# Around the first leaf of a blocked factorisation: the last key sums earlier, the upper columns of T cleared by ScalarE, three places for a

## The reference

```python
def attn(x, ...):                      # x: 8 batches, 1024 tokens, 256 wide; H = 128
    Q, K, V = x@Wq.T+bq, x@Wk.T+bk, x@Wv.T+bv
    def step(carry, qkv):              # scan over the 1024 tokens
        A, M = carry                   # A starts as the identity, M as zero, both HxH
        q, k, v = qkv
        s_t = sum(k * q)
        u = k / (norm(k) + 1e-6)
        Au = A @ u
        denom = 1.0 + u @ Au
        A = A - outer(Au, Au) / denom
        z = Au / denom
        M = M + outer(v, s_t * z)
        return (A, M), M @ q
    return scan(step) @ Wo.T + bo
x = x + 0.5 * ffn(layernorm(x))        # ffn: ternary weights, 256 -> 1024 -> 256, exact gelu
x = x + attn(layernorm(x))
x = x + 0.5 * ffn(layernorm(x))
```

## Time and profile before

| | |
|---|---|
| median of 3 runs | 1112.4 us (1110.78 to 1113.61) |
| the profiled execution | 1110.24 us, its span 1108.5 us |
| busy: PE, DVE, ACT, POOL | 940.0, 792.9, 532.3, 301.5 us |
| mean granted clock of PE | 0.917 of full speed |
| HBM read, written | 49.16 MB, 37.75 MB |
| key blocks, up to the last product of the last block | 0 to 312.7 us |
| first leaf, from `take` to `turned` | 319.86 to 369.94 us |
| second leaf | 376.85 to 419.39 us |
| third, fourth leaf | 428.0 to 470.6, 480.3 to 522.8 us |
| second part of the program | from 537.7 us |

### The profile page before, as it was taken

One profiled execution on the slowest core, in us unless ns is written; L12 is line 12 of the kernel. 1 busy time (PEld: TensorE's weight loads), 2 busy tenths in 40 slices (PEclk: granted clock), 3 DMA queues, 4 the chain that ended last, 5 costly groups with the idle time before them and its releaser, 6 DMA issues.

```text
span 1108.5 us, 28517 instructions
## 1 busy us (share of the span) xinstructions
PE 940.0 (85%) x11675; PEld 724.5 (65%) x11675; DVE 792.9 (72%) x2503; ACT 532.3 (48%) x1093; POOL 301.5 (27%) x256
## 2 busy tenths in 40 slices
PE   4799999999985877577899546692799999999998
PEld 1467777777773756465797435582667777777766
DVE  6877777777667897968359797886366666566663
ACT  4678788787733133112226212101175666566574
POOL 4345353535210000000000000000664654546340
PEclk9999999999998788778999686896799999999999
DMA  5353547545236463244443000057542433424231
GB/s 154 67 133 98 152 114 191 119 138 139 85 120 191 124 138 104 59 118 115 109 130 106 3 3 4 4 155 155 152 91 73 106 96 82 120 67 106 57 77 58
DMA packets 185522, 113.98 MB, mean 103 GB/s; under 512 B 85808, under 2 KB 178352, under 8 KB 184752
## 3 DMA queue, kind: packets, MB, share of 16 engines
q1 hardware_dynamic: 168496, 95.38, 34.1%
q10 hardware_dynamic: 16896, 16.78, 4.9%
HBM read 49.16 MB, written 37.75 MB: 78 GB/s over the span
## 4 chain that ended last, share of the span: by engine, by line
PE 32%; DVE 15%; issue 2%; DMA 1%; POOL 1%; ACT 1%; SPq 0%; DVEq 0%; ACTq 0%; POOLq 0%
PE ldl_work L2027 10%; PE ldl_work L2015 10%; DVE ldl_lane_matrix L1151 6%; DVE ldl_rank_one L1148 4%; DVE lane_rows L1133 2%; PE ldl_work L1999 2%; DVE ldl_lane_dinv L1136 2%; PE ldl_work L1594 2%; PE ldl_work L1604 1%; PE ldl_work L1982 1%; PE ldl_work L1990 1%; PE ldl_work L1983 1%; PE ldl_work L1969 1%; PE ldl_work L1411 1%; PE ldl_work L1404 1%
## 5 line engine op out<-in xcount | busy, mean ns | idle before, releaser
L1780 POOL TENSOR_TENSOR T<-T,out_bv_rows 128x512 f32<-128x512 f32 x16 | 20.3, 1272 | 430.5 <-DMA out_bv_rows<-in_bqkv 424.3
L445 DVE TENSOR_TENSOR ffn_h_rest<-ffn_ps_h,ffn_h_high 128x512 f16<-128x512 f32 x128 | 86.2, 684 | 56.1 <-ACT ffn_ps_h L616 55.6
L615 ACT ACTIVATE ffn_h_high<-ffn_ps_h,b_columns 128x512 f16<-128x512 f32 x128 | 87.9, 687 | 64.6 <-PE ffn_ps_h L694 64.1
L2027 PE MATMUL ldl_work<-w_ternary,ldl_panels 128*128 128x256 f16 x512 | 118.2, 273 | 0.0
L708 PE MATMUL ffn_ps_y<-w_ternary,ffn_h_rest 128*128 128x256 f16 x512 | 117.8, 273 | 0.0
L708 PE MATMUL ffn_ps_y<-w_ternary,ffn_h_high 128*128 128x256 f16 x512 | 117.8, 273 | 0.0
L694 PE MATMUL ffn_ps_h<-ffn_xT_high,w_ternary 128*128 128x512 f16 x256 | 98.7, 385 | 11.8 <-DVE ffn_h_rest L445 11.8
L694 PE MATMUL ffn_ps_h<-ffn_xT_rest,w_ternary 128*128 128x512 f16 x256 | 98.3, 384 | 0.0
L2015 PE MATMUL ldl_work<-out_xT_high,w_ternary 128*128 128x512 f16 x256 | 97.0, 379 | 0.0
L2015 PE MATMUL ldl_work<-out_xT_rest,w_ternary 128*128 128x512 f16 x256 | 97.0, 379 | 0.0
L1928 ACT ACTIVATE ldl_work<-ldl_work,b_columns 128x512 f32<-128x512 f32 x128 | 84.2, 658 | 0.0
(11 more groups left out here) (215 smaller groups left out, 2301.3 us busy)
## 6 DMA issues: line engine op xcount, KB each, us to landing
ffn_x<-in_x SPq DMA_DIRECT2D x16, 512.0 KB, 4.7
x_scratch<-ffn_x_out ACTq DMA_DIRECT2D x16, 512.0 KB, 3.3
aT_scratch<-ffn_aT SPq DMA_DIRECT2D x16, 512.0 KB, 5.0
inv_aT<-aT_scratch SPq DMA_DIRECT2D x16, 512.0 KB, 4.9
ldl_panels<-uT_scratch SPq DMA_DIRECT2D x32, 256.0 KB, 2.9
T<-x_scratch SPq DMA_DIRECT2D x16, 512.0 KB, 3.8
uT_scratch<-ffn_uT SPq DMA_DIRECT2D x16, 256.0 KB, 5.3
inv_uT<-uT_scratch SPq DMA_DIRECT2D x16, 256.0 KB, 4.1
```

The costliest lines, as they stand in the source:

```text
L445: nc.vector.tensor_tensor(hl[n % 2][:, f], ps_h[f % 3][:], hh[n % 2][:, f], ALU.subtract).then_inc(hl_done, 1)
L615: nc.scalar.activation(hh[n % 2][:, f], ps_h[f % 3][:], ACT.Gelu, bias=c.b1[:, f:f + 1])
L2027: ins = nc.tensor.matmul(ps_y[t % 2], part[k % 2][:, f, t * P:(t + 1) * P], c.w2[:, f], start=(f == 0 and part is hh), stop=(f == FC - 1 a ...
```

## The change

Four things are changed.

1. *The sums and the first diagonal blocks.* `prefix(E - 2)` and `prefix(E - 1)` stood at the end of DVE's key work; they now stand among the work of the last block. On PE, `product(E, pe, 0)` now comes behind `diagonal(0)`.
2. *Other keys' work in the leaf.* On ACT `squares(E + 1)` moves from behind `qv(2)` to ahead of `empty(0, "panel")`, `scale_u(E + 1)` ahead of `qv(3)`; on DVE `invert(E + 1)` moves from pivot 12 to pivot 10. On SP `load_u(0)` is issued ahead of `store_a(E + 1)` and `store_u(E - 1)`.
3. *T's upper columns.* The three transfers of `clear()` go; ACT copies the zeros in three instructions, one in each of r = 1, 2, 3, right behind `next_block(r - 1)` and the small `minus_dinv`.
4. *Three places for a.* `aT` has NA = 3 places, the third in the space "last", which grows by 5120 bytes; three are loaded ahead, and `load(n)` waits for `v_made` of group n - 3 in place of n - 2.

```diff
         store_a(E, sp)
         store_u(E - 2, sp)
-        store_a(E + 1, sp)
-        store_u(E - 1, sp)
 
         sp.wait_ge(xl_done, NBLOCK)
         sp.wait_ge(turned[1], 32 * NBLOCK // 2)
         sp.wait_ge(y_done, BT * (NBLOCK - 1))
+        e.inverse.load_u(sp, 0)
+        store_a(E + 1, sp)
+        store_u(E - 1, sp)
...
+                if f == 5 and n == NALL - 1:
+                    prefix(E - 2, v)
                 if f == 6:
                     on(n + 2, stats)
             on(n - 1, finish, BT - 1)
             on(n - 1, row_stats, BT - 1)
+            if n == NALL - 1:
+                prefix(E - 1, v)
             on(n - 1, aggregate)
-        prefix(E - 2, v)
-        prefix(E - 1, v)
...
             turn_a(E, pe, 1)
-            product(E, pe, 0)
 
             pe.wait_ge(kk_done, NSUM)
         elif part == 1:
+            product(E, pe, 0)
             product(E, pe, 1)
...
         elif part == 2:
             copy_uT(E, act)
+            squares(E + 1, act)
         elif part == 3:
-            squares(E + 1, act)
+            scale_u(E + 1, act)
         else:
-            scale_u(E + 1, act)
             copy_uT(E + 1, act)
...
-        elif pivot == 12:
+        elif pivot == 10:
             invert(E + 1, v)
...
-        for s in range(2):
+        for s in range(NA):
             keys.a_stored(sp, s)
             sp.dma_start(aT[s][:], m.aT[s]).then_inc(a_in[s], 16)
...
         def load(n):
-            s = n % 2
+            s = n % NA
             keys.a_stored(sp, n)
-            if n > 1:
-                sp.wait_ge(v_made, n - 1)
+            sp.wait_ge(v_made, n - NA + 1)
             sp.dma_start(aT[s][:], m.aT[n]).then_inc(a_in[s], 16)
...
-                    if n + 2 < NSTEP:
-                        load(n + 2)
+                    if n + NA < NSTEP:
+                        load(n + NA)
                     store_v(n)
                     if n < 2:
                         keys.last_sync(sp, n)
-                    if n == QV_OF[1][0]:
-                        keys.all_stored(sp)
-                        clear()
...
+        def clear(i):
+
+            zeros = c.ident[block_of(i), after(i)]
+            copy(m.T[block_of(i), :, after(i)], zeros.unsqueeze(1).to_broadcast([W, NP, P - W * (i + 1)])
+                 ).then_inc(cleared, 1)
...
+            if first and 0 < r < NW:
+                clear(r - 1)
             for what, n in beside(r):
```

More of the change, by code:

```diff
@@ L883, in factorise @@
         bq = sb("bq_column", [P, 1])
-        aT = [sb(f"aT{s}", [P, HC, DC, P], F32, "raw") for s in range(2)]
+        NA = 3
+        aT = [sb(f"aT{s}", [P, HC, DC, P], F32, "raw" if s < 2 else "last") for s in range(NA)]
         uT = sb("uT", [P, QV_MAX, HC, P], F32, "u")
@@ L908, in factorise @@
     e.rows_in = [stored] * 4 if first else [sem(f"last_rows_in{q}") for q in range(4)]
-    e.stored, e.all_stored = stored, 16 * (8 * NW + (NW - 1 if first else 0))
+    e.stored, e.all_stored = stored, 16 * 8 * NW
     if first:
         w_in = sem("wqv_in")
-        a_in = [sem(f"aT_in{s}") for s in range(2)]
+        a_in = [sem(f"aT_in{s}") for s in range(NA)]
         u_in = sem("uT_in")
@@ L996, in beside, with load_u @@
         return zip_longest(fills_of(r), QV_OF[r] if first and r < NW else ())
+    def load_u(sp, r):
+        if r and QV_OF[r]:
+            sp.wait_ge(dots_done, sum(1 for y in QV_OF[:r] if y))
+        for n in QV_OF[r]:
+            keys.u_stored(sp, n)
+            sp.dma_start(uT[:, slot(n)], uT_v[n]).then_inc(u_in, 16)
     def first_loads(sp):
@@ L1008, in load @@
         def load(n):
-            s = n % 2
+            s = n % NA
             keys.a_stored(sp, n)
-            if n > 1:
-                sp.wait_ge(v_made, n - 1)
+            sp.wait_ge(v_made, n - NA + 1)
             sp.dma_start(aT[s][:], m.aT[n]).then_inc(a_in[s], 16)
-        def load_u(r):
-            if r and QV_OF[r]:
-                sp.wait_ge(dots_done, sum(1 for y in QV_OF[:r] if y))
-            for n in QV_OF[r]:
-                keys.u_stored(sp, n)
-                sp.dma_start(uT[:, slot(n)], uT_v[n]).then_inc(u_in, 16)
         def store_q(n):
@@ L1056, in keep_rows @@
                                  ).then_inc(e.rows_in[q] if r == NW - 1 else stored, 16)
-        def clear():
-            for i in range(NW - 1):
-                zeros = c.ident[block_of(i), after(i)]
-                sp.dma_start(m.T[block_of(i), :, after(i)],
-                             zeros.unsqueeze(1).to_broadcast([W, NP, P - W * (i + 1)])).then_inc(stored, 16)
         def fetch_q():
@@ L1070, in fetch_q @@
                 sp.dma_start(m.KK[:, pairs], m.qT[pairs].rearrange("n i j -> i n j")).then_inc(stored, 16)
-        if first:
-            load_u(0)
         for r in range(NW + 1):
@@ L2058, in keys_and_inverses @@
         sizes = {"Y": NW * NQ * P * 4, "raw": 16384, "Z": NQ * P * 4, "u": 14336, "q": 14336,
-                 "last": 26624}
+                 "last": 31744}
         at = nc.sbuf_base + -nc.sbuf_base % 32
```

9 lines of the change are left out of this document (5 added, 4 removed).

## The result

| | median of 4 | range | ratio to before |
|---|---|---|---|
| before (same chip) | 1111.59 us | 1110.24 to 1113.61 | |
| changed | 1097.71 us | 1097.50 to 1098.47 | 0.9875 [0.9857, 0.9892] |

Faster by 13.9 us. The profiled execution took 1098.47 us with a span of 1096.8 us, 11.7 us less than before.

A forecast was written before the change was run, and what follows sets the result against it. It took the first part's chain through DVE, with PE's finish_diagonal between leaves, as the bound. -3.96 - 5.19 - 1.14 = -10.29 us gave 1099.95 for that execution, median 1102.1 us; range 1099.5 to 1103.8, with rivals 1099.0 to 1105.5.

The forecast's parts named there:

- The start: From the last feed-forward product to the first take: earlier sum and diagonal blocks make take start 3.96 us earlier.
- The 0.09 us taken for the semaphore: At the start: estimated delay from the last feed-forward product's end at 312.66 to gram at 312.75.
- Rival (a): At the start: slow clock stays or group 14 is late, gain 1.9 in place of 3.96, 1104.2 us; chance 0.20.
- The wait in the leaf: First leaf: DVE's wait before the reciprocal of group 15 goes because ACT's squares come earlier, -5.19 us.
- The lateness of `finish_diagonal(2)`: End of second leaf: qv(9) no longer waits, so finish_diagonal(2) follows turned by 0.14 us, -1.14 us.
- ScalarE's clearing: ACT's three copies of zeros, at most 7.2, 4.8 and 2.4 us, hidden in idle time: cost 0 on the path.
- The fetching: PE's issue gaps in the middle of finish_diagonal: taken as unchanged, 0 us, since quiet queues don't help by themselves.
- The bound of -1.4: Good-side bound of the fetching term: the most that shrinking issue gaps in finish_diagonal were allowed to gain, in us.
- a second part of another length: Program behind the barrier: expected to move as a whole, as long as before; a changed length would show the prediction wrong.
- the bounds of the fetching: Issue gaps in finish_diagonal: from -1.4 to +3.1 us, the latter a gap of 1.40 becoming one of 4.53.
- rival (d): First leaf: ACT's squares wait for something unseen, 2 to 4 us of the 5.19 stay, 1105 us; chance 0.06.

The follow-up runs named there:

- part 2 alone: Kernel before plus only the other keys' work moved in the leaf and u loaded ahead of the two stores, still two places for a: 1103.19 us, 0.9953.
- t_traffic2: Changed kernel plus eight useless 512 KB stores, four near the end of each of the first two leaves, in flight as finish_diagonal starts: 1101.08 us, 0.9918.
- m1_late_sums: Changed kernel with the last two sums and the first diagonal blocks put back where they were: 1099.52 us, 0.9907.
- b_busy: Changed kernel plus 128 useless small matmuls on PE ahead of finish_diagonal(1) and another 128 ahead of (2): 1097.54 us, 0.9897.

## Why the prediction came out as it did

**The start: right, -3.96 predicted, -4.01 measured** (7.20 to 3.19 us). The 0.09 us taken for the semaphore was 0.10. But 1.6 us of the gain is not the reordering, and that the size came out is luck to that extent. The profiled execution of before had the slow clock there (0.62 granted in the earlier trace rows); four kernels with the old order have 5.60 us, and one of them 1.06 and 1.08 us for the two rows. The granted clock of the changed kernel is 1.00 from 315 to 317 us. Rival (a), the slow clock stays, did not occur in any trace of a kernel with part 1. How often the slow clock occurs with the old order is open: 1 of 5 traces.

**The wait in the leaf: right, -5.19 predicted, -5.26 measured.** The reasoning by ACT's queue holds: part 2 alone gives 44.82 us. That the places remove most of the same wait was in the rows (ACT was queued behind a `qv(2)` that waited for its a), but the prediction didn't draw it.

**The lateness of `finish_diagonal(2)`: right, -1.14 predicted, -1.14 measured** (1.28 to 0.14 us behind `turned`). ScalarE's clearing cost nothing, as said.

**The fetching: wrong, "I take 0".** This is the step that failed. The stretch to the second take lost 1.63 us and that to the third 1.67 us beyond the lateness: together -3.3 us. That is the fall of the two gaps, 1.40 and 2.41 to 0 and 0.24 us, less 0.3 us that the rest of the two stretches took more. The premise was read from one row: the gap of 2.00 us in a stretch with a DMA share of 0.03 showed, I said, that quiet queues don't help. It shows that a gap remains when they are quiet, because in the third `finish_diagonal` blocks end inside dense streams; it says nothing about how much of a gap elsewhere is delay by data. The comparison to make was 2.41 and 4.53 us in busy stretches against 1.75 and 2.00 us in quiet ones (the first gap, 1.40 us at pair 26 of a half, would have gone the other way). The bound of -1.4 was also too short, since it counted only the first of the two gaps on the path; the sentence before it had named the second. That the queues would be quieter at these moments could have been drawn from the steps themselves (three clearing transfers gone, loads earlier); how quiet, only the traces told. The packets and t_traffic2 show it.

**The sum.** With the last two stretches (-0.26 to the fourth take, -0.64 behind the fourth leaf) the first part shortened by 14.6 us. The profiled spans differ by 11.7 only: in the changed execution the key blocks took 0.8 us more (313.45 against 312.66) and the second part 2.1 us more. I find no cause for these in the change: m1_late_sums has both, too (313.65 and 573.11 us), but b_busy and t_traffic2, which contain the whole change, have a second part of 571.05 and 570.82 us. The prediction named a second part of another length as a sign of being wrong; by itself it doesn't tell, since it differs by up to 3.6 us from trace to trace. The medians differ by 13.9. The forecast took 10.3, and set it against a median of 1112.4 us of three runs; with the fourth it is 1111.59. Two things in its range don't follow from its own terms: the bounds of the fetching, -1.4 and +3.1, with 1.5 us of spread would have made 1099.2 to 1106.7, and rival (d), at 1104.1 to 1106.1, has no part in 1109.1 to 1115.7.

**Left open.** Why a gap of some 1.8 us stands even with quiet queues was not taken apart. In the third `finish_diagonal` of the changed kernel the packet comes in 458.5 to 459.0, some 0.9 us behind the start of the stream at 457.84, and PE returns at 461.14, 3.30 us behind it; the 94 pairs before the gap cover 1.58 us, and 1.72 are left. So a packet and some 2.4 us after it have to fit into the work that PE has left; what triggers the request, and what takes those 2.4 us, no run shows. Nor is it known why the second gap of the third `finish_diagonal` is 1.75 to 1.80 us in six kernels, 2.1 to 2.35 in five and 0.20 in two. Whether the small gaps in the second part's factorisation can be shifted in the same way wasn't tried.

## What to carry to other kernels

When an engine waits for "issue" in the middle of a dense stream of small instructions, look in the DMA queues for the instruction packet and what runs beside it: a transfer moved away from there, or a few dummy instructions that shift the block's end into idle time, may be worth as much as a wait removed. Before pricing parts of a change one by one, ask which of them remove the same wait: here the four alone promised 18 us and gave 14, and an earlier start alone gave nothing, as the next waits took it. And check a duration of the stretch that you price against the same instructions elsewhere in the trace, since one execution may hold a slow clock that others don't.
